# Attention on one Trainium2 core: where the projection unit, the sums of the probabilities and K's low part stand in a step

## What is computed

```python
h   = layernorm(x) * (1 + ca) + sa              # ca, sa, ga: one vector per batch
qkv = h @ W_qkv + b_qkv                         # 128 -> 16 heads x (64 q, 64 k, 64 v)
attn = softmax(Q @ K.T / 8)                     # 1024 x 1024 for each of 4 x 16 heads
x   = x + ga * ((attn @ V) @ W_fc + b_fc)
```

## Time and profile before

| | |
|---|---|
| runs | 1831.11 us median (1827.95 to 1837.15) |
| profiled execution | 1838.18 us, span 1836.5 us |
| a pair of heads in the loop | 47.4 us |
| PE, DVE, ACT, POOL busy | 88%, 64%, 51%, 62% of the span |
| waits of VectorE's reductions for maxima (L633) | 174.9 us |
| idle time of PE in front of maxima (L810) | 112.9 us, 105.2 of it until VectorE's L633 |
| mean granted TensorE clock | 0.963 |

### The profile page before, as it was taken

The page is one execution under the profiler, slowest core; times in us unless marked ns, Lnnn a source line. Parts: engine busy times, 40 slices in busy tenths (PEclk is TensorE's granted clock), DMA queues, the critical chain, the costliest instruction groups (busy, mean ns, idle before and its releaser), DMA issues. The chain is left out here.

```text
span 1836.5 us, 29420 instructions
## 1 busy us (share of the span) xinstructions
PE 1616.6 (88%) x8907; PEld 857.5 (47%) x8907; DVE 1171.9 (64%) x2591; ACT 928.5 (51%) x1369; POOL 1136.6 (62%) x517
## 2 busy tenths in 40 slices
PE   4699989999999999999999999999999998756996
PEld 3344444444444444444444444444444444244886
DVE  5567656666666666666666666666666665287887
ACT  3354545555545555555555555555555454325874
POOL 3177666776676667666776777667666766520134
PEclk8699999999999999999999999999999999857999
DMA  2001000000000000000000000000000000110010
GB/s 88 16 24 30 30 30 29 29 29 29 25 18 23 27 29 29 29 29 29 29 24 28 29 29 29 29 29 29 29 29 29 29 25 14 40 47 23 30 35 29
DMA packets 60737, 54.40 MB, mean 30 GB/s; under 512 B 23677, under 2 KB 46746, under 8 KB 60698
## 3 DMA queue, kind: packets, MB, share of 16 engines
q1 hardware_dynamic: 60544, 53.90, 9.4%
q10 hardware_dynamic: 154, 0.03, 0.0%
HBM read 31.35 MB, written 2.36 MB: 18 GB/s over the span
## 5 line engine op out<-in xcount | busy, mean ns | idle before, releaser
L526 POOL TENSOR_TENSOR ACC<-ACC,PR 128x1024 f32<-128x1024 f32 x382 | 913.2, 2391 | 276.2 <-ACT PR L590 259.2
L633 DVE TENSOR_REDUCE NMH<-ps_mx 128x1 f32<-128x512 f32 x1024 | 657.6, 684 | 174.9 <-PE ps_mx L810 174.5
L590 ACT ACTIVATE PR<-ps_s 128x1024 f32<-128x1024 f32 x512 | 497.1, 1023 | 323.3 <-PE ps_s L834 320.9
L845 PE MATMUL ps_o<-PR,V 128*64 128x512 f32 x2048 | 492.7, 602 | 0.0
L810 PE MATMUL ps_mx<-KH,QH 64*128 64x512 f32 x1024 | 256.8, 496 | 112.9 <-DVE NMH L633 105.2
L526 POOL TENSOR_TENSOR ACC<-PR 128x1024 f32<-128x1024 f32 x64 | 151.3, 2365 | 206.9 <-ACT PR L590 206.9
L810 PEld LDWEIGHTS ps_mx<-KH,QH 64*128 64x128 f32 x1024 | 97.6, 185 | 321.1 <-DVE NMH L633 181.9
L845 PEld LDWEIGHTS ps_o<-PR,V 128*64 128x64 f32 x2048 | 129.8, 136 | 232.0 <-issue 197.0
L831 PE MATMUL ps_s<-QH,DL 64*128 64x512 f32 x1024 | 204.1, 391 | 0.0
L834 PE MATMUL ps_s<-QL,DH 64*128 64x512 f32 x768 | 152.9, 390 | 0.0
L828 PE MATMUL ps_s<-QH,DH 64*128 64x512 f32 x768 | 152.8, 391 | 0.0
(11 more groups left out here) (195 smaller groups left out, 2032.8 us busy)
## 6 DMA issues: line engine op xcount, KB each, us to landing
hcur<-hT SPq DMA_DIRECT2D x32, 512.0 KB, 3.3
SUM<-recip_rows SPq DMA_DIRECT2D x128, 128.0 KB, 2.9
Wraw<-in_L_attn_W_qkv SPq DMA_DIRECT2D x32, 192.0 KB, 2.9
x<-in_L_attn_X SPq DMA_DIRECT2D x4, 512.0 KB, 5.3
Wfc<-in_L_attn_W_fc SPq DMA_DIRECT2D x32, 64.0 KB, 2.3
R<-SUM SPq DMA_DIRECT2D x128, 2.0 KB, 1.8
hT<-in_L_attn_X SPq DMA_DIRECT2D x4, 512.0 KB, 6.2
out<-e_res SPq DMA_DIRECT2D x7, 256.0 KB, 2.3
```

Source lines behind the costliest of these rows:

```text
L526: G.tensor_tensor(ACC[:, ch, :, :], a, PR[:, t, :, :], ALU.add).then_inc(added, 1)
L590: A.activation(PR[:, t, :, :], ps_s[:, t % 2, :, :], ACT.Exp, scale=SCALE).then_inc(exp_done, 1)
L633: D.tensor_reduce(NMH[:, ch, h, i, kc:kc + 1], ps_mx[:, h, :], AX, ALU.max, negate=True).then_inc(mx_red, 1)
L845: last = T.matmul(ps_o[half(h), :], V[:, u, t, half(h)], PR[:, t, h, :], start=(t == 0), stop=(t == 7))
```

## The change

In every step the unit stands between the second `maxima` and `times_v`, not at the end. `sums` stand at the end of steps 3 and 7 (5 for the last pair), ahead of `rows`, and write bank 1 of `ps_mx`: they wait for the reductions of the second `maxima`, and the first `maxima` of steps 4 and 0 waits for ScalarE's copy of them. `LATE`, `RECIP` and `NORM` change accordingly: chunk 0's output projection moves to step 3 of the next pair. ScalarE reads a unit right behind the step's exponentials, ahead of `copy_o` and `split_w`, and K's high part `KH` is now written there; `DH` stays at the head of the next step with a semaphore of its own (`k_dh`). VectorE does both reductions in a row, then the first part of the unit and the normalisation; K's second part comes ahead of the next step's reductions.

The tables:

```diff
-        LATE = {0: ("k", 1, 0), 1: ("k", 1, 1), 2: ("q", 1, 0), 3: ("q", 1, 1), 4: ("v", 1, 0), 5: ("fc", -1, 1),
-                6: ("v", 1, 1), 7: ("fc", 0, 0)}
-        SUMS = {3: (-1, 1), 5: (0, 0)}
-        RECIP = {4: (-1, 1), 6: (0, 0)}
-        NORM = {5: (-1, 1), 7: (0, 0)}
+        LATE = {0: ("k", 1, 0), 1: ("k", 1, 1), 2: ("q", 1, 0), 3: ("fc", -1, 0), 4: ("q", 1, 1), 5: ("v", 1, 0),
+                6: ("v", 1, 1), 7: ("fc", -1, 1)}
+        RECIP = {1: (-1, 0), 5: (-1, 1)}
+        NORM = {2: (-1, 0), 6: (-1, 1)}
...
+        def sums_at(n, d):
+            if d == 3 and has(n - 1):
+                return n - 1, 1
+            if d == (5 if isinstance(n, int) and n == NP - 1 else 7):
+                return n, 0
+            return None
```

SyncE, in `pair`:

```diff
                 if has(n - 1):
+                    compact_sums(n - 1, 0)
+                    spread_recip(n - 1, 0)
                     compact_sums(n - 1, 1)
                     spread_recip(n - 1, 1)
-                compact_sums(n, 0)
-                spread_recip(n, 0)
```

ScalarE, in `early_part` for K:

```diff
                     A.activation(Kraw[:, q], ps_w[:, :], ACT.Identity, bias=bias[:, u, 1:2]).then_inc(k_raw, 1)
+                    act.wait_ge(k_raw, 2 * m + ch + 1)
+                    A.activation(KH[:, u, q], Kraw[:, q], ACT.Copy).then_inc(k_hi, 1)
```

ScalarE, in `pair`:

```diff
                 for d in range(8):
-                    x = late_at(n, d - 1)
+                    done = sums_at(n, d - 1) if d else has(n - 1) and (n - 1, 0)
+                    if done:
+                        sums(*done)
+                    x = late_at(n, u, d - 1)
                     if x:
-                        late_part(x[0], x[1], parity(u, LATE[(d - 1) % 8][1] - (d == 0)), x[2])
+                        late_part(*x)
                     exponentials(n, 2 * d)
                     exponentials(n, 2 * d + 1)
+                    x = late_at(n, u, d)
+                    if x:
+                        early_part(*x)
                     if d == 4:
                         copy_o(n, 0)
                     if d == 0 and has(n - 1):
                         copy_o(n - 1, 1)
```

VectorE, in `pair`:

```diff
+                    if d in RECIP and has(n + RECIP[d][0]):
+                        invert(n + RECIP[d][0], RECIP[d][1])
+                    x = late_at(n, u, d - 1)
                     if x:
-                        early_part(*x)
+                        late_part(*x)
                     k = 2 * d + 9
                     if has(group(n, u, k)[0]):
                         reduce_max(*group(n, u, k), 16 * n + k)
+                    if has(group(n, u, k + 1)[0]):
+                        reduce_max(*group(n, u, k + 1), 16 * n + k + 1)
+                    x = late_at(n, u, d)
                     if x:
-                        late_part(*x)
+                        early_part(*x)
                     if d in NORM and has(n + NORM[d][0]):
                         normalise(n + NORM[d][0], NORM[d][1])
```

TensorE, in `sums` and `pair`:

```diff
+            def sums(m, ch, groups):
                 pe.wait_ge(added, 14 * m + 7 * ch + 7)
+                wait(pe, sums_in, 2 * m + ch)
+                wait(pe, mx_red, 2 * groups)
                 for h in range(2):
-                    last = T.matmul(ps_w[half(h), :], g.ones[:, 0:64], ACC[:, ch, h, :], start=True, stop=True)
+                    last = T.matmul(ps_mx[half(h), 1, :], g.ones[:, 0:64], ACC[:, ch, h, :], start=True, stop=True)
...
                         if d % 4 == 0:
                             pe.wait_ge(neg_rows, 2 * n + d // 4 + 1)
+                            wait(pe, sums_in, 2 * n - 1 + d // 4)
...
                         maxima(*group(n, u, k + 1), 16 * n + k + 1)
-                    if d in SUMS and has(n + SUMS[d][0]):
-                        freed(previous(n, d, True))
-                        sums(n + SUMS[d][0], SUMS[d][1])
+                    x = late_at(n, u, d)
+                    if x:
+                        freed(before(n, u, d))
+                        unit(*x)
                     if d:
                         times_v(n, u, 2 * d - 2)
                         times_v(n, u, 2 * d - 1)
...
+                    if sums_at(n, d):
+                        sums(*sums_at(n, d), groups)
                     if d % 4 == 3 and has(group(n, u, k)[0]):
...
                         rows(m, ch)
-                    x = late_at(n, d)
-                    if x:
-                        before = previous(n, d, False)
-                        if before:
-                            freed(before)
-                        unit(x[0], x[1], parity(u, LATE[d][1]), x[2])
```

More of the change, by code:

```diff
@@ L403, in has, with late_at @@
             return not isinstance(n, int) or 0 <= n < NP
-        def late_at(n, d):
+        def late_at(n, u, d):
             if d < 0:
-                return late_at(n - 1, d + 8)
+                return late_at(n - 1, 1 - u, d + 8)
             kind, off, ch = LATE[d]
-            return (kind, n + off, ch) if has(n) and has(n + off) else None
+            return (kind, n + off, parity(u, off), ch) if has(n) and has(n + off) else None
+        def sums_at(n, d):
[4 more added lines that the diff above has]
+            return None
         def parity(u, off):
@@ L492, in last @@
             def last():
+                compact_sums(NP - 1, 0)
+                spread_recip(NP - 1, 0)
                 compact_sums(NP - 1, 1)
@@ L559, in late_part @@
                     return
-                q = slice(ch * 512, ch * 512 + 512)
                 new = slice(256 - 256 * ch, 512)
-                act.wait_ge(k_raw, 2 * m + ch + 1)
-                A.activation(KH[:, u, q], Kraw[:, q], ACT.Copy)
                 act.wait_ge(k_step, 2 * m + ch + 1)
-                A.activation(DH[:, u, ch * 512 + new.start:ch * 512 + 512], ps_w[:, new], ACT.Copy).then_inc(k_hi, 1)
+                A.activation(DH[:, u, ch * 512 + new.start:ch * 512 + 512], ps_w[:, new], ACT.Copy).then_inc(k_dh, 1)
             def sums(m, ch):
@@ L712, in pair @@
                         reduce_max(*group(n, u, k), 16 * n + k)
+                    if has(group(n, u, k + 1)[0]):
+                        reduce_max(*group(n, u, k + 1), 16 * n + k + 1)
+                    x = late_at(n, u, d)
                     if x:
-                        late_part(*x)
-                    if d in RECIP and has(n + RECIP[d][0]):
-                        invert(n + RECIP[d][0], RECIP[d][1])
+                        early_part(*x)
                     if d in NORM and has(n + NORM[d][0]):
                         normalise(n + NORM[d][0], NORM[d][1])
-                    if has(group(n, u, k + 1)[0]):
-                        reduce_max(*group(n, u, k + 1), 16 * n + k + 1)
                     if d == 6 and has(n + 2):
@@ L745, in last @@
             def last():
-                early_part("fc", NP - 1, 1, 0)
+                invert(NP - 1, 0)
                 for t in range(LAST_ON_POOL, 8):
@@ L796, in freed @@
             def freed(x):
-                kind, m, ch = x
-                pe.wait_ge({"k": k_lo, "q": q_lo, "v": v_copied, "sums": sums_in, "fc": fc_added}[kind], 2 * m + ch + 1)
+                kind, m, _, ch = x
+                pe.wait_ge({"k": k_lo, "q": q_lo, "v": v_copied, "fc": fc_added}[kind], 2 * m + ch + 1)
             def maxima(m, u, ch, i, kc, count):
@@ L850, in first @@
                 unit("k", 0, 0, 0)
-                freed(("k", 0, 0))
+                freed(("k", 0, 0, 0))
                 unit("k", 0, 0, 1)
-                freed(("k", 0, 1))
+                freed(("k", 0, 0, 1))
                 unit("q", 0, 0, 0)
@@ L870, in first, with before @@
                 rows(0, 0)
-            def previous(n, d, sums_now):
-                if not sums_now and d in SUMS and has(n + SUMS[d][0]):
-                    return ("sums", n + SUMS[d][0], SUMS[d][1])
-                k = d - 1
-                while True:
-                    x = late_at(n, k) if k >= 0 or has(n - 1) else None
+            def before(n, u, d):
+                for k in range(d - 1, d - 9, -1):
+                    x = late_at(n, u, k)
                     if x:
                         return x
-                    e = k % 8
-                    j = n + k // 8
-                    if e in SUMS and has(j) and has(j + SUMS[e][0]):
-                        return ("sums", j + SUMS[e][0], SUMS[e][1])
-                    if k < -8:
-                        return None
-                    k -= 1
+                return ("v", 0, 0, 1)
             def pair(n, u):
@@ L891, in pair @@
                     k = 2 * d + 9
+                    groups = min(16 * n + k + 2, 16 * NP) if isinstance(n, int) else 16 * n + k + 2
                     if has(group(n, u, k)[0]):
@@ L908, in pair @@
                         times_v(n - 1, 1 - u, 15)
+                    if sums_at(n, d):
+                        sums(*sums_at(n, d), groups)
                     if d % 4 == 3 and has(group(n, u, k)[0]):
                         m, _, ch, _, _ = group(n, u, k)
```

(15 more changed lines are left out.)

21 lines of the change are left out of this document (9 added, 12 removed).

## The result

The changed kernel takes 2030.24 us (median of 4 runs, 2017.88 to 2034.23) against 1833.38 us (1827.95 to 1837.15): ratio 1.108, interval 1.104 to 1.112. The forecast was 1842 with a range from 1816 to 1864. The sign of the forecast was right, the size was not: +197 us where +11 were expected.

What follows compares the result with a forecast made beforehand. TensorE, busy 88% of the span, was taken to bound the kernel. Thirty pairs at 1.96 us added less 1.29 removed (+20), -1.4 for pair 0 and -7.9 for late copies made +11 us: 1842 us, range 1816 to 1864.

Steps and rivals of the forecast that it cites:

- Unit ahead of the products, reductions at once: Second maxima: VectorE reduces at once, leaving waits of 0.14 us in steps 3, 5, 6, none in 0 and 4.
- K's low part, and the copy of O ahead of `DH`: Steps 1 and 2: VectorE finishes DL, behind ScalarE's DH, before reducing; the second maxima waits 1.4 and 0.69 us.
- The rival in which the copy of O holds nothing: Step 1: last products ready early, a wait of 0.33 us, 1.07 less in 30 pairs, 1810 us; chance 12%.
- The unit out of the shadow: Steps 3 and 7: units no longer run beside the mask; TensorE gets 0.90 + 1.06 = 1.96 us more a pair.
- The copy of the sums: Behind the rows of steps 3 and 7: ScalarE's copy takes 0.6 us, covered by the 1.19 us there; no cost.
- So steps with nothing else ahead of the reduction keep 0.14 us: Step 3, among others: the second maxima waits only 0.14 us for VectorE's reduction.
- about 0.8 us into step 7, 0.3 late as an estimate: a wait of 0.44: Step 7: VectorE's 1.25 us of subtractions end late, so the second maxima waits 0.44 us, bounds 0 and 0.6.
- The clock rival: Idle times of 1.3 us in step 1 and 0.9 behind rows lower the clock: 1888 or 1865 us; chance 11%.
- The late copy: Normalisations in pairs 3 and 30 no longer wait for late spread reciprocals: -7.9 us, bounds 0 and -8.

Runs made afterwards that it cites:

- experiment 4: The changed kernel with ScalarE's copy of O for chunk 1 moved behind K's DH at the head of step 1: 1981.6 us, ratio 1.083.
- experiment 7: The changed kernel with the units of steps 3 and 7 back behind the rows, read by VectorE behind the mask: 1934.6 us, ratio 1.057.
- experiment 1: The changed kernel with the normalisation cut to 8 of 512 columns and the low-part subtraction to 2 of 64 per head: 1870.4 us, ratio 1.022.
- experiment 2: The changed kernel with only the normalisation cut to 8 of 512 columns, the weights' low part whole: 1922.6 us, ratio 1.050.
- experiment 3: The kernel before the change with only VectorE's normalisation moved behind both reductions: 1876.8 us, ratio 1.026.
- experiment 5: The changed kernel with the normalisation and the weights' low-part subtraction moved from VectorE to GpSimd's own list: 1834.2 us, ratio 1.002.
- experiment 6: The changed kernel with the products of one key tile moved ahead of the second maxima in steps 3 and 7: 1891.5 us, ratio 1.034.
- three small repairs: The changed kernel with the edits of experiment 4, experiment 5 and experiment 7 together: 1746.8 us, ratio 0.953 against the kernel before.

## Why the prediction was wrong

The steps of the sum, against the changed kernel and the runs:

- *Unit ahead of the products, reductions at once:* right. The second maxima comes 1.88 us behind the first in steps 5 and 6 and without a wait in steps 0 and 4, as worked out.
- *K's low part, and the copy of O ahead of `DH`:* right in mechanism and size. Step 1 was to have its second maxima at 3.1 us and has it at 3.09; step 2 at 2.43 and has 2.32. The rival in which the copy of O holds nothing is refuted by the timeline and by experiment 4 (1.11 us a pair):

```profile
616.75 1.94 PE L859 MATMUL ps_o<-PR,V 128*64 128x512 f32 x8
...
618.62 0.50 PE L824 MATMUL ps_mx<-KH,QH 64*128 64x512 f32 x2
...
618.74 0.60 ACT L583 ACTIVATE O<-ps_o 128x512 f32<-128x512 f32 x1 [0.53 <-PE ps_o L859]
...
619.23 0.38 ACT L573 ACTIVATE DH<-ps_w 128x256 fp32r<-128x256 f32 x1
...
619.65 0.48 DVE L679 SCALAR_TENSOR_TENSOR DL<-ps_w,bias,KH 128x256 fp32r<-128x256 f32 x1 [1.47 <-ACT DH L573]
...
621.71 0.50 PE L824 MATMUL ps_mx<-KH,QH 64*128 64x512 f32 x2 [1.20 <-DVE NMH L642]
```

- *The unit out of the shadow:* right. The gap behind the rows is the full distance, with idle times of 1.08 us ahead of step 0 and 0.79 ahead of step 4, and experiment 7 prices a unit at about 1.0 us. From the rows to the maxima the forecast had 1.19 us, 0.1 more or less; the trace has 1.11 ahead of step 4 and 1.42 ahead of step 0, outside the bound, for a reason that no run shows:

```profile
611.84 0.33 PE L807 MATMUL ps_mx<-ident_r,NM 128*128 128x128 f32 x1
...
612.32 0.69 DVE L652 TENSOR_TENSOR BQ<-ps_mx,mask 128x512 fp32r<-128x512 f32 x1 [3.95 <-PE ps_mx L807]
...
613.26 0.49 PE L824 MATMUL ps_mx<-KH,QH 64*128 64x512 f32 x2 [1.08 <-DVE BQ L652]
```

- *The copy of the sums* never ended last behind the rows: VectorE's mask is named, not ScalarE.
- *"So steps with nothing else ahead of the reduction keep 0.14 us"*, said of step 3, and of step 7 that VectorE's subtractions end *"about 0.8 us into step 7, 0.3 late as an estimate: a wait of 0.44"*: **this is the step that failed.** I moved two VectorE instructions in time and kept their durations. In the changed kernel they end 2.3 and 2.7 us into steps 3 and 7. In its place the runs show that an instruction of VectorE with both inputs in SBUF waits until GpSimd's running addition, whose inputs are in SBUF too, is done (experiments 1, 2, 3). It costs 1.66 and 2.04 us of TensorE's time a pair and brings two falls of the clock of 1.67 us, and with both instructions on GpSimd the time is 1834 (experiment 5).
- *The clock rival* (11%, 1865 to 1888) had the second mechanism, but put the trigger at the gaps of 1.3 and 0.9 us. Alone, those never brought it down in the loop (experiments 5 and 6). Behind the gaps of 1.66 and 2.04 us, which come from the hold-up, it fell twice in each of the pairs 5 to 29. A fall was priced rightly: 1.5 us forecast, 1.67 measured.
- *The late copy:* I took the 2.02 us of the earlier trace rows for a wait for the DMA. The row's own bracket gives the DMA 1.27 us of idle time *before* it; the 2.02 are the instruction's length, and an addition of GpSimd was running. The row held the very effect that I missed. The term itself came out: in the changed kernel no normalisation before the last pair waits for its DMA.

Per pair the account closes: steps 3 and 7 take 21.67 us in the changed kernel and 14.70 in experiment 5. Of the 6.97 us, 1.66 + 2.04 = 3.70 are idle time for the hold-up and two falls of the clock are 3.34, together 0.07 too many. The 25 pairs 5 to 29 lose this, 174 us in all, and the pairs around them the rest with fewer falls; between the two kernels as a whole lie 196 us. Without the hold-up the forecast would have been met (1842 against 1834). The 8 us between them are about the size of one term, the subtraction's wait in step 7: in experiment 5, where VectorE no longer has it, the second maxima comes at 1.88 us there and the forecast had 2.18, 9 us in 30 pairs. The smaller misses, 0.16 us too much in steps 1 and 2 and 0.15 too little behind the rows, nearly cancel, which is luck.

What the trace of before shows, and the prediction does not read, is GpSimd's row beside the normalisation's and the subtraction's:

```profile
444.55 0.68 DVE L684 TENSOR_TENSOR O<-O,SUM 128x512 f32<-128x512 f32 x1
...
445.25 4.80 POOL L526 TENSOR_TENSOR ACC<-ACC,PR 128x1024 f32<-128x1024 f32 x2 [2.62 <-ACT PR L590]
...
451.32 4.96 POOL L526 TENSOR_TENSOR ACC<-ACC,PR 128x1024 f32<-128x1024 f32 x2 [1.27 <-ACT PR L590]
...
452.80 1.25 DVE L624 TENSOR_TENSOR Wlo<-Wraw,Whi 128x128 fp32r<-128x128 f32 x2
```

The normalisation ends at 445.23 and the addition starts at 445.25. It ran in a gap of GpSimd, and was done 20 ns before the gap's end. The two subtractions took 1.25 us, though one of them takes 0.28 (shortest 277 ns, median 285, longest 1069): the first had met an addition. The Trainium skill states the rule, in "SBUF — State Buffer" (Who interferes with whom): a VectorE instruction with two SBUF inputs contends with a GpSimd instruction that reads SBUF, the later one blocks until the first is done, and one with at most one SBUF input does not contend, outside the modes in which it uses two ports. By this rule and the change's new order the hold-up could have been foretold. The traces agree: 8 columns took 2.13 us, the sum with one input in PSUM its usual 0.68, and GpSimd's two additions in experiment 3 took 5.12 us when the second of them started during the normalisation.

What stays open is when the clock falls. In the loop it never fell behind gaps of 1.2 us, behind gaps of 1.5 us twice in 25 pairs, and behind those of 1.7 and 2.0 us 50 times in 25 pairs of the changed kernel, but only 35 times in experiment 4 and 23 in experiment 7, where the same gaps stand in a shorter pair. The length of the gap is thus not all of it, and no run varied its place in time alone.

## What to carry to other kernels

A duration in a trace belongs to a place: before moving a VectorE instruction with both inputs in SBUF, look at what GpSimd does at its new place, and at its old one. Its shortest and longest duration in the trace tell whether it is sensitive (277 ns to 1069 ns here). If the new place collides, give the instruction to GpSimd's own list (experiment 5), or put other work of the waiting engine into the gap (experiment 6), before giving up the order.

Take a rearrangement apart before judging it: here three small repairs turned 11% slower into 5% faster.

## What the runs showed that I had not expected

- A VectorE multiplication of 128x8 took 2.13 us behind a GpSimd addition of 2.4, the one of 128x512 up to 2.66: the wait, not the work.
- A fall of the clock costs 1.67 us here, about as much as the wait ahead of it, and so nearly doubled the price of the two long gaps.
- The same step with the same waits has a fall in one pair and none in the next (experiment 4).
- One tile of products alone takes 1.0 us, two in a row 1.87.
